# Moving scaling work to VectorE, a second stage buffer and a fetch on GpSimd's queue, in a two-layer graph kernel

## The reference

```
edge_index = jnp.stack([src, dst])
h = jnp.maximum(_layernorm(x), 0.0)
x = x + (segment_sum((h @ W0)[src] * edge_weight[:, None], dst) + b0)
h = jnp.maximum(_layernorm(x), 0.0)
xt = jnp.einsum('ni,rio->rno', h, W1)          # 8 relations
x = x + relu(segment_sum(xt[edge_type, dst], src) + b1)
```

## Time and profile before

| | |
|---|---|
| median of three executions | 1354.59 us (1352.87 to 1359.52) |
| the profiled execution, its own time | 1354.78 us |
| its span | 1353.0 us |
| PE busy | 1026.3 us (76%) |
| DVE busy | 1017.9 us (75%) |
| POOL busy | 916.5 us (68%) |
| ACT busy | 772.1 us (57%) |

### The profile page before, as it was taken

How to read it: one execution, slowest core, us unless ns; L and a number is a source line. 1 busy time by engine, 2 the same in 40 slices (tenths; PEclk the granted TensorE clock), 3 DMA queues, 4 the chain that set the end, 5 groups by cost and what they waited for, 6 DMA issues and landing times.

```text
span 1353.0 us, 25033 instructions
## 1 busy us (share of the span) xinstructions
PE 1026.3 (76%) x5291; PEld 738.2 (55%) x5291; DVE 1017.9 (75%) x3498; ACT 772.1 (57%) x2116; POOL 916.5 (68%) x919
## 2 busy tenths in 40 slices
PE   2588767778778857889899999677777667677766
PEld 2477656656566735667677777444444433333433
DVE  8899769999898898778687765777777765555554
ACT  4899948889788446767677753676766500000000
POOL 1587847777777677666566540777777777777775
PEclk9799979999999979999999999899999987877786
DMA  4011123333333654455556584333333334444442
GB/s 140 2 26 34 30 77 102 101 99 100 105 101 103 90 158 132 148 174 157 156 152 188 152 144 139 100 104 104 105 106 105 105 108 118 116 121 117 116 121 87
DMA packets 83474, 150.16 MB, mean 111 GB/s; under 512 B 18262, under 2 KB 56756, under 8 KB 83380
## 3 DMA queue, kind: packets, MB, share of 16 engines
q0 software_dynamic: 42336, 109.27, 31.1%
q1 hardware_dynamic: 41044, 39.77, 8.8%
HBM read 115.90 MB, written 32.99 MB: 110 GB/s over the span
## 4 chain that ended last, share of the span: by engine, by line
PE 31%; DVE 20%; issue 12%; POOL 11%; ACT 11%; DMA 10%; DVEq 3%; ACTq 0%; POOLq 0%; SPq 0%
POOL rows L428 11%; PE bank L1250 10%; DMA rows<-table,idx 8%; ACT oh_f L468 8%; PE bank L1269 8%; PE bank L1402 7%; PE bank L1241 5%; DVE x_sb L884 4%; DVE oh_m L869 3%; DVE oh_t L819 3%; DVE oh_p L809 2%; DVEq L876 1%; DMA x_sb<-in_x_dram 1%; DVE scan L637 1%; DVE oh_m L872 1%
## 5 line engine op out<-in xcount | busy, mean ns | idle before, releaser
L412 POOL DMA_INDIRECT rows<-table,idx_ring x440 | 437.2, 994 | 197.6 <-issue 118.3
L428 POOL DMA_INDIRECT rows<-table,idx x392 | 374.6, 956 | 163.3 <-issue 99.7
L1269 PE MATMUL bank<-rows,oh_m 128*128 x880 | 331.7, 480 | 138.9 <-DMA rows<-table,idx 64.5
L1250 PE MATMUL bank<-rows,oh_m 128*128 128x256 f32 x880 | 282.9, 407 | 113.1 <-DVE x_sb L884 111.7
L884 DVE TENSOR_TENSOR x_sb<-x_sb,bank 128x256 f32 x880 | 362.9, 412 | 7.4 <-PE bank L1269 5.2
L1241 PE MATMUL bank<-oh_t,oh_f 125*128 125x220 bf16 x2425 | 345.3, 261 | 13.8 <-ACT oh_f L468 10.0
L468 ACT ACTIVATE oh_f<-oh_p,ew_part 125x128 bf16<-125x128 f16 x850 | 324.8, 689 | 28.5 <-DVE oh_p L809 25.6
L1241 PEld LDWEIGHTS bank<-oh_t,oh_f 125*128 125x128 f16 (+1 forms) x2425 | 261.1, 118 | 100.4 <-ACT oh_f L468 16.4
L468 ACT ACTIVATE oh_f<-oh_p,hi 125x128 f16<-125x128 f16 x400 | 269.9, 675 | 79.6 <-DVE oh_p L809 79.5
L1269 PEld LDWEIGHTS bank<-rows,oh_m 128*128 128x128 f32 x880 | 159.0, 218 | 268.7 <-issue 260.9
L468 ACT ACTIVATE oh_f<-oh_p,lo 125x128 f16<-125x128 f16 x400 | 271.3, 678 | 0.0
(11 more groups left out here) (220 smaller groups left out, 750.1 us busy)
## 6 DMA issues: line engine op xcount, KB each, us to landing
table<-stage SPq DMA_DIRECT2D x100, 256.0 KB, 2.4
rows<-table,idx_ring POOLq DMA_INDIRECT x440, 2.9
rows<-table,idx POOLq DMA_INDIRECT x392, 2.8
table<-stage SPq DMA_DIRECT2D x25, 128.0 KB
x_sb<-in_x_dram SPq DMA_DIRECT2D x1, 3072.0 KB
out_dram<-done_first SPq DMA_DIRECT2D x20, 128.0 KB
w_sb<-in_L_gnn_weight_dram SPq DMA_DIRECT2D x2, 1024.0 KB, 15.6
scattered<-pay,place POOLq DMA_INDIRECT x75
```

Of the source, the lines that this page charges most:

```text
L412: pool.indirect_dma_start(out=rows[:, u, :], out_offset=None, in_=table0[:, :], in_offset=bass.IndirectOffsetOnAxis(ap=idx_ring[:, u:u + 1 ...
L428: pool.indirect_dma_start(out=rows1[:, g % RR, :], out_offset=None, in_=table1[:, :], in_offset=bass.IndirectOffsetOnAxis(ap=idx[s % 2][:, ...
L1250: TE.matmul(message_bank(u), oh_m[:, u % OR, :], rows[:, u, :], start=True, stop=True).then_inc(s_msg, 1)
L1269: TE.matmul(message_bank(u), oh_m[:, u % OR, :], rows1_flat[:, ds(slot, D)], start=True, stop=True).then_inc(s_msg, 1)
```

## The change

Three edits in sort 0 and the table of layer 0.

1. From column 75 on (`MORE`), VectorE also makes field 3, as one product for a group (L824 after), and ScalarE makes field 4 alone.
2. `stage0` has two buffers, used in turn; each has its semaphore. ScalarE waits for the store of the block before the last. SyncE's loop over the blocks is written out.
3. The fetch of `back` goes from SyncE's queue, behind the 25 table stores, to GpSimd's, behind the 75 scatters. It waits for the same semaphores.

The rest, numerical result included, is as before.

```diff
+    MORE = 75
...
-        stage0 = sb_over("rows", "stage0", [P, D], f32, off=(2 + 2 * TU) * D * 4)
-        rest0 = (3 + 2 * TU) * D * 4
+        stage0 = sb_over("rows", "stage0", [P, 2, D], f32, off=(2 + 2 * TU) * D * 4)
+        rest0 = (4 + 2 * TU) * D * 4
...
-            with sp.Fori(0, NB) as b:
+            for b in range(NB):
                 sp.wait_ge(s_staged, b + 1)
-                sp.dma_start(table0[ds(b * P, P), :], stage0[:, :]).then_inc(s_stored0, 16)
-            sp.wait_ge(s_scat, 16 * CQ)
-            sp.wait_ge(s_h[0], 2)
-            sp.wait_ge(s_x1, 2)
-            sp.dma_start(back[:, :, :].rearrange("p t k -> p (t k)"), back_rows).then_inc(s_back, 16)
+                sp.dma_start(table0[b * P:(b + 1) * P, :], stage0[:, b % 2, :]).then_inc(s_stored0[b % 2], 16)
...
-            pool.wait_ge(s_stored0, 16 * NB)
+            pool.wait_ge(s_scat, 16 * CQ)
+            pool.wait_ge(s_h[0], 2)
+            pool.wait_ge(s_x1, 2)
+            pool.dma_start(back[:, :, :].rearrange("p t k -> p (t k)"), back_rows).then_inc(s_back, 16)
+
+            for k in range(2):
+                pool.wait_ge(s_stored0[k], (NB + 1 - k) // 2 * 16)
...
-                fields = {0: ((3, ew_part[1]), (4, ew_part[2])),
-                          1: ((2, ew_part[0]), (3, ew_part[1]), (4, ew_part[2])),
-                          2: ((0, hi32[0]), (1, lo32[0])),
-                          3: ((0, hi32[1]), (1, lo32[1]))}[s]
+                if s == 0:
+                    fields = ((4, ew_part[2]),) if cols >= MORE else ((3, ew_part[1]), (4, ew_part[2]))
+                elif s < CH:
+                    fields = ((2, ew_part[0]), (3, ew_part[1]), (4, ew_part[2]))
+                else:
+                    fields = ((0, hi32[s - CH]), (1, lo32[s - CH]))
...
-                        if b:
-                            act.wait_ge(s_stored0, b * 16)
-                        nc.scalar.activation(stage0[:, :], bank_t0(b), ACT.Copy).then_inc(s_staged, 1)
+                        if b > 1:
+                            act.wait_ge(s_stored0[b % 2], b // 2 * 16)
+                        nc.scalar.activation(stage0[:, b % 2, :], bank_t0(b), ACT.Copy).then_inc(s_staged, 1)
...
                 if s == 0:
                     V.tensor_tensor(into[2][:, r, :, :], places[:, r, :, :], over_places(ew16[0], c), ALU.mult)
+                    if c >= MORE:
+                        V.tensor_tensor(into[3][:, r, :, :], places[:, r, :, :], over_places(ew16[1], c), ALU.mult)
```

More of the change, by code:

```diff
@@ L56, in gnn_kernel @@
     FIRST = [b * 9 // 2 for b in range(NB)]
-    assert CP % G == 0 and FIRST[-1] < CP
+    MORE = 75
+    assert CP % G == 0 and MORE % G == 0 and FIRST[-1] < CP
     READY = [(EP * CC + (P - 1) * NB) * (k + 1) // (NB * P) for k in range(NB)]
@@ L313, in gnn_kernel @@
         s_staged = sem("s_staged")
-        s_stored0 = sem("s_stored0")
+        s_stored0 = [sem(f"s_stored0_{k}") for k in range(2)]
         s_stored1 = [sem(f"s_stored1_{u}") for u in range(SG)]
```

## The result

| | before | after |
|---|---|---|
| median | 1354.99 us (9 executions) | 1348.47 us (9 executions, 1347.25 to 1351.46) |
| ratio, 95% interval | | 0.9947, 0.9931 to 0.9963 |
| span of the profiled execution | 1353.0 us | 1346.8 us |
| merge of the scattered columns | 180.87 us | 173.03 us |

The account below looks back on a forecast made before the run. It took ScalarE with its table stores, then the fetch behind them on SyncE's queue, as the bound. Afterwards the scatter chain puts the merge at 174.6 against 180.87: 1354.78 - 6.3 = 1348.5 us, range 1344.7 to 1353.5.

Parts of the forecast that it names:

- The gate: End of first sort: GpSimd's scatters and the fetch become the bound, with the merge at 174.6 us against 180.87.
- theory A: Follow-up theory: merge starts when the last of three chains ends: scatters landed and fetched, first sort read, SyncE's queue free.
- VectorE's end: First sort: VectorE's last oh_t tile ends 2.3 us later, at 165.5 instead of 163.2; sort readable at about 167.6.
- both filled waits: VectorE in the first sort: waits of 0.9 us for block order and 1.5 us for the tile row absorb added products.
- The buffers: Layer 0 table: second stage buffer removes four ScalarE store waits, 7.0 us; worth at most 3.4 us by itself.
- The sum of the scatter chain: Before the merge: scatters landed 170.0, plus 1.2 stretch, 0.1 restart, 3.2 fetch and 0.1, giving 174.6 us.
- the 1.2 us for ten products: Scatters in the first sort: ten added VectorE products lengthen them by 0.12 us each, bounds 0 and 4.7 us.
- scatters not stretched: Rival, 17%: products do not hold GpSimd's scatters; gain 7.5 to 8.2 us, time 1346.6 to 1347.3 us.
- Pass-through: From the merge to the kernel's end: the 6.3 us gained at the merge reach the end in full.
- lost later: Rival, 7%: part of the gain goes into longer waits in phase 0; 3 us of gain kept, 1351.8 us.
- The clock: Rival, 6%: TensorE starts phase 0 at 1.2 GHz and stays there, losing 0.5 us per us; 40 us give 1368.5.
- The rule on the shared port: VectorE beside scatters: by the rule the ten products would be free, 1347.3 us; the prediction held the trace against it.

Follow-up runs that it names:

- the fetch alone: Changed kernel with one stage buffer and all field scalings back on ScalarE; only the fetch of `back` stays on GpSimd's queue: 1349.55 us, ratio 0.996.
- the delay: Changed kernel with 25 chained VectorE copies of 0.31 us each added right after the merge: 1356.56 us, ratio to the kernel before 1.0007.
- all but the fetch: Changed kernel with the fetch of `back` put back on SyncE's queue behind the 25 table stores: 1348.92 us, ratio 0.9949.
- scaling alone: Changed kernel with one stage buffer and the fetch back on SyncE's queue; only field 3's move to VectorE stays: 1348.8 us, ratio 0.995.
- buffers alone: Changed kernel with all scalings back on ScalarE and the fetch back on SyncE's queue; only the second stage buffer stays: 1349.0 us, ratio 0.9946.
- all but the scaling: Changed kernel with all scalings back on ScalarE; two stage buffers and the fetch on GpSimd stay: 1348.49 us, ratio 0.9955.
- early places: Changed kernel with VectorE's positions and scatter places computed ahead of the splitting of the edge weights: 1346.14 us, ratio 0.994.
- more products: Changed kernel with VectorE making field 3 in all 25 groups, 15 products more: 1349.8 us, ratio 0.9962.
- early places, two products fewer: Changed kernel with scatter places computed before the edge-weight splitting and VectorE making field 3 only from column 85 on: 1347.4 us, ratio 0.9943.
- add moved: Changed kernel with the residual's starting add moved from each group's last column to its second: 1345.7 us first, 1347.3 us as second run's median (ratio 0.9937).
- both together: Changed kernel with scatter places computed before the edge-weight splitting and the residual's add at each group's second column: 1346.83 us, ratio 0.9928.

## Why the prediction was right

The forecast was 1348.5 us, the result 1348.47. Part of that is luck: two deviations cancel.

*The gate.* Confirmed by the chain, which runs through the scatters and the fetch, and by five runs that each put one or two of the three edits back and moved the merge to within 0.7 us of where theory A had put it beforehand. One of them, the fetch alone, showed a further bound: with one stage buffer the table stores hold the first gather behind the merge. In the changed kernel they do not, as the prediction says.

*VectorE's end.* Last oh_t tile forecast at 165.5, measured 165.43; both filled waits are gone. TensorE's last weight product started 0.8 us later than forecast (166.33 against 165.5), and the sort was read at 168.35 instead of 167.6. Nothing hung on it.

*The buffers.* No ScalarE wait for a store, as forecast, in the profiled execution; with the delay, whose code is the same up to the merge, there was one of 3.5 us. Off the path, as forecast, both times.

*The sum of the scatter chain* is where sizes were off. The last scatter started at 167.12, not at 168.75: the 1.2 us for ten products was wrong. The kernel without them, with the other two edits, starts its last scatter at 166.98, 0.14 us earlier, and with 15 more it starts at 166.59. From there to the fetch 3.06 us passed, not 2.55; 2.55 is what SyncE takes (all but the fetch), and no row of before had GpSimd waiting for a scatter. The fetch was ready 2.85 us after its issue, not 3.3. Together -1.63 + 0.51 - 0.45: the merge at 173.03, 1.6 us ahead of 174.6. The rival "scatters not stretched" was the better account of this term: it put the merge between 172.7 and 173.4. The sign "merge at 174 to 175" did not come.

*Pass-through.* Against 7.84 us at the merge stand 6.2 us in the spans and 6.5 us in the medians. I had assumed no loss. The distance from the merge to the end of the span, by kernel:

| kernel | merge | span | from merge to end |
|---|---|---|---|
| before | 180.87 | 1353.0 | 1172.1 |
| after | 173.03 | 1346.8 | 1173.8 |
| scaling alone | 172.86 | 1345.9 | 1173.0 |
| buffers alone | 175.40 | 1347.2 | 1171.8 |
| fetch alone | 175.90 | 1345.5 | 1169.6 |
| all but the fetch | 172.26 | 1343.5 | 1171.2 |
| all but the scaling | 173.03 | 1347.1 | 1174.1 |
| early places | 169.71 | 1344.0 | 1174.3 |
| more products | 176.55 | 1351.0 | 1174.5 |
| early places, two products fewer | 171.30 | 1350.3 | 1179.0 |
| add moved, first execution | 170.53 | 1343.9 | 1173.4 |
| add moved, second | 170.63 | 1345.8 | 1175.2 |
| both together | 170.78 | 1345.3 | 1174.5 |

The code behind the merge is the same in all, and the distance varies by up to 9.4 us with no order in it; two executions of one kernel, with the add moved, differ by 1.8. In the profiled pair the shift is 7.9 us at the first gather, 6.7, 5.1 and 4.6 at the reads of sorts 1 to 3 and 6.2 at the end, so it is not even along the way either. The 1.6 us between before and after lies inside that, the run with the delay gave its 7.8 us back in full, and the interval of the ratio (5.0 to 9.3 us) holds 7.84. So a loss is not shown. The rival "lost later" finds no support, but a loss of 1 to 2 us could not be seen. Since the merge came 1.6 us earlier than forecast and the span kept 1.6 us less of it than the merge gained, the two cancel in the number; that is the luck.

*The clock.* TensorE's granted clock was 0.66 in 180 to 200 us of both kernels, a mix of its two levels, and 1.00 after, against 0.92 before, in 200 to 220. It did not stay at 1.2 GHz: the slower rival did not happen.

*The rule on the shared port.* The Trainium skill (SBUF — State Buffer, "Who interferes with whom") infers that a tensor_tensor with two SBUF inputs does not hold up the writing of descriptors. For the added fifth product the runs agree: it cost the scatters nothing. For the rest they do not bear the rule out: in the changed kernel ten scatters end 1.61 us after their group's first product, where the third product ends, and these ten hold 6.2 of the 11.5 us above 75 x 1.19. These products are tensor_tensors with two SBUF inputs. A scatter also reads its places out of SBUF (`place`), and the rule as the prediction tells it does let such an instruction meet GpSimd work that reads SBUF; no run separates that reading from the writing of descriptors. I used the row of 1.89 us against the rule and spread the excess evenly over the products. The even spread was the mistake; which instructions hold a scatter is open.

## What to carry to other kernels

Before pricing an edit, list every chain that must end before the next stage and when each ends: the gain is at most the distance to the next chain that the edit leaves alone, and three edits of 8.0, 5.5 and 5.0 us alone gave 7.8 together. The scaling alone would have done. List the chains of the stage after as well: with the fetch alone the merge gained 5.0 us and the first gather 2.8. When the critical queue has been relieved, ask at once what releases it next; here it was a row of scatters whose start stood behind six instructions nobody needed yet, and moving the scatters' places ahead of them was worth another 3.3 us at the merge, 2.3 of it by the earlier start and the rest by less stretched scatters. A cost averaged over a mixed background (the 11.9 us of stretch over 100 products) is no price of one more instruction of it.

## What the runs showed of the hardware

- A scatter's length depends on where in VectorE's group it starts. In the kernel after (timeline of GpSimd):

```profile
126.32 2.27 POOL L399 DMA_INDIRECT scattered<-pay,place  x1 [0.30 <-issue]
...
131.94 1.63 POOL L399 DMA_INDIRECT scattered<-pay,place  x1 [0.30 <-issue]
...
147.90 1.47 POOL L399 DMA_INDIRECT scattered<-pay,place  x1 [0.30 <-issue]
149.66 1.19 POOL L399 DMA_INDIRECT scattered<-pay,place  x1 [0.30 <-issue]
```

  The first two end at 128.59 and 133.57, both 1.61 us after their group's first product (126.98 and 131.96; the one-hot `oh_p` counts as the first), though the one started 0.66 us before it and the other with it. Ten of the 75 end there. The third ends 2.21 us after its group's first product (147.16); eight end at this point. It lies inside the fifth product, which began at 149.15, but scatters of the kernel before, with four products in a group, end there too: one at 122.82, 2.20 us after 120.62. So some seem to be held up to fixed points within the group, and a fifth product adds nothing. The other stretched ones end elsewhere, under scans and tile instructions. No run took one of the first four products away.
- A plain transfer on GpSimd's queue (220 KB) took 0.60 us of the engine and landed 2.76 us after its start, against 0.33 and 2.45 us on SyncE's. With early places it took 3.5 us, with table stores under way at the same time.
- The small scatter is slow to be done, for 125 pieces of 8 bytes. From the start of the last one to the start of the fetch that waited for it 3.06 us passed on GpSimd's queue in the changed kernel (2.8 to 3.1 in the other kernels that fetch there, 4.3 once), and 2.55 us on SyncE's.
